# Two self-attention layers on one core: the softmax tiles of the first layer made in two halves of 512 queries

## The chip, the cores and the metric

The kernel runs on 1 core of a Trainium2 chip, in one launch. The metric is the device time of one execution in microseconds. TensorE multiplies matrices, ScalarE evaluates functions and copies, VectorE and GpSimd do elementwise work, and SyncE issues the DMAs. The engines run their own instruction streams and wait for each other only on semaphores.

## The reference

There are 8 images of 256 channels and 32 x 32 = 1024 positions, in fp32. Two layers follow each other, and each adds its result to its input:

```python
# layer 0 (q and k have 32 channels)
q = einsum('oc,bcn->bno', Wq, x) + bq
k = einsum('oc,bcn->bon', Wk, x) + bk
v = einsum('oc,bcn->bon', Wv, x) + bv
attn = softmax(einsum('bnc,bcm->bnm', q, k), axis=-1)
x = gamma * einsum('bcj,bij->bci', v, attn) + x
# layer 1 (256 channels), on the group norm h of x (32 groups)
attn = softmax(einsum('bct,bcs->bts', q(h), k(h)) / sqrt(256), axis=-1)
y = x + proj(einsum('bcs,bst->bct', v(h), attn))
```

## The kernel before

**Numbers.** Nearly every product is made of values split into a high part (`fp32r`) and a low part (the rest), as three matmuls that add into one bank: high x high, high x low, low x high (`three`, lines 597 to 599). The high part is written by ScalarE, the low part by VectorE, or by GpSimd for some operands.

**Layer 0.** An image has 8 tiles of 128 positions. In a first pass, `scores`, TensorE makes a 128 x 1024 tile of energies with queries on the partitions (line 607). VectorE takes each row's negated maximum (`row_max`, line 1067), and ScalarE the sum of the exponentials (`row_sums`, line 844), written back over the tile. From both comes one shift for each query (`log_sums`, `shifts`), which goes into two extra rows of the query matrix. In the second pass, `keys`, TensorE makes the tile again with keys on the partitions and the shift added (line 617), so that the exponential of it is already the transposed, normalised probability. This is a **keys tile**. ScalarE takes the exponential into `prob` (`exponent`, line 820) and copies it to `pt_hi` (`prob_hi`, line 834), and VectorE subtracts into `pt_lo` (`prob_lo`, line 1084), each over 1024 queries in one instruction. `prob` has 3 buffers, `pt_hi` and `pt_lo` have 4 each.

**Values.** `values` multiplies a tile's probabilities with 128 rows of v. It adds into four PSUM banks, numbered by `bank_of`: banks 0 and 1 are the two channel tiles for the first 512 queries, banks 2 and 3 those for the last 512. Each bank takes three matmuls.

**Layer 1.** Its tile, `logits`, is made once (12 matmuls). Its exponential has a row maximum as bias and gives the row sum. High and low part are scaled by the row's inverse.

**PSUM.** `ring` has four slots of 1024 columns. Slots 2 and 3 are the four banks of `values`. Slots 0 and 1 are handed round among everything else: keys, scores and logits tiles, and the projections `qk`, `value0`, `query` and `value1`. A table worked out at the start gives each entry its slot and the entry that had it before (`BEFORE`). Ahead of a fill, `wait_read` waits until that earlier entry has been read. For a keys tile this is the semaphore `keys_exp`, for scores `scores_exp`, for `query` `query_split`.

**Order.** `STEPS` is written by hand. A step has at most one tile, the `values` of a tile two steps back, and other entries. TensorE fills the step's tile, then its `early` entries, then makes the first `banks_first` banks of `values`, fills the `sides`, makes the remaining banks, and fills the `late` entries. Images 2 to 7 are made in one turn of 16 steps each, `turn(i)`: 8 keys tiles of image i, then 8 logits tiles of image i - 1. In steps 4 to 7 of a turn, where there is a next image, the order on TensorE is: keys tile, scores tile of image i + 1, banks 0 and 1, then one projection of image i - 1 (`query` 0 and 1, `value1` 0 and 1), then banks 2 and 3. The keys and scores tiles take the two slots, and the projection takes the slot of that step's keys tile. Step 3 makes `qk` of the next image right after its keys tile, in the slot of the keys tile of step 2. ScalarE's order in a step is: keys tile (exponential, copy), early entries (`row_sums`), sides, late entries. In step 1 it also makes the high part of layer 1's input (`hidden`, line 810).

The lines that decide when a slot is free, of `fill` and `reader`:

```python
if before and not (kind == before[0] == "weights"):
    wait_read(before)
...
"scores": ("scores_exp", image * TILES + m + 1),
"keys": ("keys_exp", image * TILES + m + 1),
"qk": ("qk_split", image * 2 + m + 1),
```

Of the kernel before, what the change touches and what calls it, by code (L numbers as in the profile page):

```python
# [6 lines left out]
F32 = mybir.dt.float32  # L7
F32R = mybir.dt.float32r
ACT = mybir.ActivationFunctionType
# [4 lines left out]
CT = C // P  # L14
TILES = N // P
# [6 lines left out]
PROBS = 3  # L22
PT = 4
# [194 lines left out]
RING_NO, SLOT, BEFORE, TILE_NO, PHASE_NO = {}, {}, {}, {}, {}  # L218
# [24 lines left out]
TILE_OF = list(TILE_NO)  # L243
# [23 lines left out]
def values_done(tile):  # L267

    kind, image, k = tile
    phase = PHASE_NO[int(kind == "logits"), image]  # L270
    if k == TILES - 1:
        return "pv_ready", phase * BANKS + BANKS
    return "tile_done", phase * (TILES - 1) + k + 1
# [1 line left out]

SEMAPHORES = (
    "ring_ready", "scores_max", "scores_exp", "log_ready", "shift_ready", "shift_read",
    "keys_exp", "logits_max", "logits_exp", "inv_ready", "p_hi", "p_split", "tile_done",
    "pv_ready", "pv_read", "query_half", "qk_hi", "qk_split", "value0_taken", "value0_kept", "value0_first", "value0_hi", "value0_split", "query_hi", "query_split",
    "v1_full", "v1_hi", "value1_split", "stats_ready", "norm_read", "coef_ready", "h_full", "h_hi", "h_split",  # L280
    "x_hi", "x_split", "res0_ready", "res1_ready", "weights_read", "weights_split", "rows_ready", "bias_read",
# [4 lines left out]
def build(nc, x, wqk_t, bqk, bk0, wv0_t, bv0, gamma, norm_w, norm_b, wq, bq, wk, bk, wv, bv, wp_t, bp,  # L286
          ident, group, y):
    with ExitStack() as ctx:
        def sb(name, shape, dt=F32):
            return ctx.enter_context(nc.sbuf_tensor(name, shape, dt))  # L290
# [16 lines left out]
        prob = sb("prob", [P, PROBS, N])  # L307
        pt_hi = [sb(f"pt_hi{j}", [P, N], F32R) for j in range(PT)]
        pt_lo = [sb(f"pt_lo{j}", [P, N], F32R) for j in range(PT)]
        neg_max = sb("neg_max", [P, 2])  # L310
        neg_raw = sb("neg_raw", [P, 2])
        row_sum = sb("row_sum", [P, 2])
        row_inv = sb("row_inv", [P, 2])
# [42 lines left out]
        ring = ctx.enter_context(nc.psum_tensor("ring", [P, 4, N], F32))  # L356
# [36 lines left out]
        def value1_split(i, k):  # L393

            if i == LAST:
                return [v[k // 4][:].rearrange("p (k c) -> p k c", c=C)[:, k % 4:] for v in (q4, k4)]
            return v1_hi[:, k:], v1_lo[:, k:]

        S = {name: ctx.enter_context(nc.semaphore(name)) for name in SEMAPHORES}
# [10 lines left out]
        half_cols = [slice(half * HALF, (half + 1) * HALF) for half in range(HALVES)]  # L410
# [167 lines left out]
        def _(pe):  # L578
            mm = nc.tensor.matmul

            def wait(name, n):
                pe.wait_ge(S[name], n)

            def wait_read(entry):

                for got in [entry] + GUESTS.get(entry, []):
                    wait(*reader(got))
                    if got[0] == "qk":
                        wait("key_hi", 2 * got[1] + got[2] + 1)
# [6 lines left out]
            def three(out, w_hi, w_lo, m_hi, m_lo, first, last):  # L596
                mm(out, w_hi, m_hi, start=first, stop=False)  # L597
                mm(out, w_hi, m_lo, start=False, stop=False)  # L598
                return mm(out, w_lo, m_hi, start=False, stop=last)  # L599
# [150 lines left out]
            def values(tile, banks):  # L750
                layer, i, k = tile
                p, phase = TILE_NO[("keys", "logits")[layer], i, k], PHASE_NO[layer, i]
                v_hi, v_lo = value1_split(i, k) if layer else (v0_hi[:, k:], v0_lo[:, k:])
                if k % 2 == 0 and 0 in banks:
                    if layer == 1:
                        wait("value1_split", 4 * i + k // 2 + 1)
                    elif i == 0:
                        wait("value0_first", k // 2 + 1)
                    else:
                        wait("value0_split", 4 * i + k // 2 - 3)  # L760
                if 0 in banks:
                    wait("p_split", p + 1)
                for b in banks:
                    half, ct = bank_of[b]
                    before = BEFORE[layer, i, 2 + b // 2] if k == 0 else None
                    if before and before[0] == "phase":
                        wait("pv_read", before[1] * BANKS + b + 1)
                    elif before and b % 2 == 0:
                        wait_read(before)
                    w, cols = slice(ct * P, (ct + 1) * P), half_cols[half]  # L770
                    last = three(pv_ps[:, b], v_hi[:, 0, w], v_lo[:, 0, w], pt_hi[p % PT][:, cols],
                                 pt_lo[p % PT][:, cols], k == 0, k == TILES - 1)
                    if k == TILES - 1:
                        last.then_inc(S["pv_ready"], 1)
                    elif b == BANKS - 1:
                        last.then_inc(S["tile_done"], 1)
# [17 lines left out]
        def _(act):  # L794
            copy, activation = nc.scalar.copy, nc.scalar.activation
# [17 lines left out]
            def exponent(tile):  # L813
                kind, i, k = tile
                p, slot = TILE_NO[tile], SLOT[tile]
                if p >= PROBS:
                    act.wait_ge(S["p_split"], p - PROBS + 1)
                if kind == "keys":
                    act.wait_ge(S["ring_ready"], RING_NO[tile] + 1)
                    activation(prob[:, p % PROBS], ring[:, slot], ACT.Exp).then_inc(S["keys_exp"], 1)  # L820
                else:
                    act.wait_ge(S["logits_max"], i * TILES + k + 1)
                    activation(prob[:, p % PROBS], ring[:, slot], ACT.Exp, bias=neg_max[:, k % 2:k % 2 + 1],  # L823
                               accum_out=row_sum[:, k % 2:k % 2 + 1]).then_inc(S["logits_exp"], 1)

            def prob_hi(tile):
                kind, i, k = tile
                p = TILE_NO[tile]
                if p >= PT:
                    name, n = values_done(TILE_OF[p - PT])  # L830
                    act.wait_ge(S[name], n)
                if kind == "keys":
                    act.wait_ge(S["keys_exp"], i * TILES + k + 1)
                    copy(pt_hi[p % PT][:], prob[:, p % PROBS]).then_inc(S["p_hi"], 1)  # L834
                else:
                    act.wait_ge(S["inv_ready"], i * TILES + k + 1)
                    activation(pt_hi[p % PT][:], prob[:, p % PROBS], ACT.Identity,  # L837
                               scale=row_inv[:, k % 2:k % 2 + 1]).then_inc(S["p_hi"], 1)

            def row_sums(entry):  # L840
                _, i, k = entry
                slot = SLOT[entry]
                act.wait_ge(S["scores_max"], i * TILES + k + 1)
                activation(ring[:, slot], ring[:, slot], ACT.Exp, bias=neg_max0[:, k:k + 1],  # L844
                           accum_out=row_sum0[:, k:k + 1]).then_inc(S["scores_exp"], 1)
# [5 lines left out]
            def shift_rows(entry):  # L851
                _, i, _ = entry
                act.wait_ge(S["ring_ready"], RING_NO[entry] + 1)
                copy(q4[i % 2][96:98], ring[0:2, SLOT[entry]]).then_inc(S["shift_read"], 1)
# [45 lines left out]

            def follow(entry):
                if entry[0] == "keys":
                    exponent(entry)
                    prob_hi(entry)
                elif entry[0] == "scores":
                    row_sums(entry)
                elif entry[0] == "shift":
                    shift_rows(entry)
                else:
                    project_hi(entry)  # L910
# [33 lines left out]
        def _(dve):  # L944
            V = nc.vector
# [11 lines left out]
            scale = C ** -0.5  # L957
# [120 lines left out]
            def prob_lo(tile):  # L1078
                kind, i, k = tile
                p = TILE_NO[tile]  # L1080
                hi, lo, src = pt_hi[p % PT], pt_lo[p % PT], prob[:, p % PROBS]
                dve.wait_ge(S["p_hi"], p + 1)
                if kind == "keys":
                    V.tensor_tensor(lo[:], src, hi[:].bitcast(F32), ALU.subtract).then_inc(S["p_split"], 1)  # L1084
                else:
                    dve.wait_ge(S["inv_ready"], i * TILES + k + 1)
                    V.scalar_tensor_tensor(lo[:], src, row_inv[:, k % 2:k % 2 + 1], hi[:].bitcast(F32), ALU.mult,  # L1087
                                           ALU.subtract).then_inc(S["p_split"], 1)
# [43 lines left out]
            def follow(entry):  # L1132
                if entry[0] == "keys":
                    prob_lo(entry)
                elif entry[0] == "scores":
                    row_max(entry)
                elif entry[0] == "norm":
                    norm(entry)
                else:
                    project_lo(entry)  # L1140
# [95 lines left out]
```

## Time and profile before

| | |
|---|---|
| time, median of 3 runs | 789.38 us (786.51 to 790.51) |
| time of the profiled execution | 785.61 us |
| its span | 783.8 us |
| TensorE busy | 774.1 us (99%), 3816 matmuls |
| VectorE busy | 554.7 us (71%), 806 instructions |
| ScalarE busy | 470.7 us (60%), 619 instructions |
| GpSimd busy | 163.8 us (21%) |
| mean granted clock of TensorE | 0.998 |

The span runs from the first instruction to the last; the time includes what lies around it. A matmul's row shows its time through the array, so rows overlap: the distance between two starts tells what one costs in the stream. An idle time in brackets is the engine's own, and the name behind the arrow is what ended it.

### The profile page before, as it was taken

Reading aid. Unit: us, or ns where it says so; the run is one execution under the profiler, and the core shown is the slowest. Engines: PE = TensorE matmul, PEld = TensorE weight load, DVE = VectorE, ACT = ScalarE, POOL = GpSimd, SP = SyncE. Lnnn points to the kernel's source line nnn. Section 1 sums busy time; section 2 is a strip of 40 time slices with the busy share of each in tenths; the row PEclk is TensorE's granted clock in tenths of the full one; section 3 lists DMA queues with packets and bytes.
Section 4 is the critical chain, followed back from the end, with each engine's and each line's share of the span. In section 5 each row is a group of like instructions: output and inputs, shape, how many; then the busy total and the mean of one; then the engine's idle time right before and its main releaser. Section 6 shows DMA issues by size and latency. Waiting matters only on the chain.

```text
span 783.8 us, 9844 instructions
## 1 busy us (share of the span) xinstructions
PE 774.1 (99%) x3816; PEld 647.4 (83%) x3816; DVE 554.7 (71%) x806; ACT 470.7 (60%) x619; POOL 163.8 (21%) x147
## 2 busy tenths in 40 slices
PE   9899999999999999999999999999999999999998
PEld 8678888888888888888888888888888888888886
DVE  5966778787578875788657796677856765476664
ACT  4876566567555775467745586456855566345343
POOL 5730052023100331005110240102310024111120
PEclk9999999999999999999999999999999999999999
DMA  6010010002000110001100011000100000000101
GB/s 189 0 55 1 1 54 1 1 23 86 1 1 1 55 54 1 1 1 54 55 1 1 0 56 54 1 1 0 54 1 2 0 33 22 1 0 1 54 1 54
DMA packets 10365, 18.98 MB, mean 24 GB/s; under 512 B 2128, under 2 KB 3920, under 8 KB 10320
## 3 DMA queue, kind: packets, MB, share of 16 engines
q1 hardware_dynamic: 10320, 18.36, 6.8%
q8 instruction: 30, 0.49, 0.3%
q14 instruction: 15, 0.12, 0.1%
HBM read 9.97 MB, written 8.39 MB: 23 GB/s over the span
## 4 chain that ended last, share of the span: by engine, by line
PE 95%; ACT 2%; DVE 2%; issue 0%; POOL 0%; ACTq 0%; DVEq 0%; POOLq 0%
PE ring L597 29%; PE ring L599 28%; PE ring L598 28%; PE ring L617 4%; PE ring L607 3%; PE ring L594 1%; ACT ring L844 1%; ACT pt_hi L834 1%; ACT prob L820 1%; PE ring L636 1%; DVE neg_max L1067 0%; DVE res L1120 0%; DVE pt_lo L1084 0%; PE ring L691 0%; PE ring L716 0%
## 5 line engine op out<-in xcount | busy, mean ns | idle before, releaser
L597 PE MATMUL ring<-pt_hi,v_hi 128*128 128x512 f32 x480 | 189.4, 395 | 0.0
L599 PE MATMUL ring<-pt_hi,v_lo 128*128 128x512 f32 x480 | 188.5, 393 | 0.0
L598 PE MATMUL ring<-pt_lo,v_hi 128*128 128x512 f32 x480 | 188.3, 392 | 0.0
L823 ACT ACTIVATE prob<-ring,neg_max 128x1024 f32<-128x1024 f32 x64 | 71.5, 1118 | 155.1 <-DVE neg_max L1070 155.1
L1069 DVE TENSOR_REDUCE neg_raw<-ring 128x1 f32<-128x1024 f32 x64 | 78.2, 1222 | 58.0 <-PE ring L599 57.9
L504 POOL TENSOR_TENSOR v_lo<-v_f,v_hi 128x512 fp32r<-128x512 f32 x28 | 37.7, 1347 | 385.1 <-ACT v_hi L861 385.1
L1084 DVE TENSOR_TENSOR pt_lo<-prob,pt_hi 128x1024 fp32r<-128x1024 f32 x64 | 81.8, 1278 | 37.5 <-ACT pt_hi L834 37.3
L599 PEld LDWEIGHTS ring<-pt_hi,v_lo 128*128 128x128 f32 x480 | 90.3, 188 | 19.9
L597 PEld LDWEIGHTS ring<-pt_hi,v_hi 128*128 128x128 f32 x480 | 90.5, 188 | 18.4 <-issue 0.4
L598 PEld LDWEIGHTS ring<-pt_lo,v_hi 128*128 128x128 f32 x480 | 90.6, 189 | 18.2
L1067 DVE TENSOR_REDUCE neg_max<-ring 128x1 f32<-128x1024 f32 x64 | 77.7, 1223 | 35.4 <-PE ring L607 35.3
L844 ACT ACTIVATE ring<-ring,neg_max 128x1024 f32<-128x1024 f32 x64 | 69.4, 1084 | 39.9 <-DVE neg_max L1067 39.8
L1087 DVE SCALAR_TENSOR_TENSOR pt_lo<-prob,row_inv,pt_hi 128x1024 fp32r<-128x1024 f32 x64 | 83.1, 1298 | 8.6 <-ACT pt_hi L837 8.4
L597 PE MATMUL ring<-h_hi,query_hi 128*128 128x512 f32 x224 | 88.0, 393 | 0.0
L598 PE MATMUL ring<-h_lo,query_hi 128*128 128x512 f32 x224 | 87.5, 391 | 0.0
L599 PE MATMUL ring<-h_hi,query_lo 128*128 128x512 f32 x224 | 87.5, 391 | 0.0
L820 ACT ACTIVATE prob<-ring 128x1024 f32<-128x1024 f32 x64 | 65.5, 1024 | 36.4 <-PE ring L617 36.2
L837 ACT ACTIVATE pt_hi<-prob,row_inv 128x1024 fp32r<-128x1024 f32 x64 | 73.7, 1152 | 9.6 <-DVE row_inv L1076 9.3
L834 ACT CAST pt_hi<-prob 128x1024 fp32r<-128x1024 f32 x64 | 67.3, 1051 | 5.3
L599 PEld LDWEIGHTS ring<-h_hi,query_lo 128*128 128x128 f32 x224 | 42.0, 188 | 8.9
L597 PEld LDWEIGHTS ring<-h_hi,query_hi 128*128 128x128 f32 x224 | 42.1, 188 | 8.8 <-ACT prob L823 0.2
L598 PEld LDWEIGHTS ring<-h_lo,query_hi 128*128 128x128 f32 x224 | 42.1, 188 | 8.6
(167 smaller groups left out, 1346.8 us busy)
## 6 DMA issues: line engine op xcount, KB each, us to landing
out_y<-res SPq DMA_DIRECT2D x32, 256.0 KB, 2.2
x_in<-in_x SPq DMA_DIRECT2D x7, 1024.0 KB, 4.9
x_in<-in_x SPq DMA_DIRECT2D x2, 512.0 KB, 5.2
h_f<-in_wv_t SPq DMA_DIRECT2D x1, 256.0 KB, 4.4
res<-in_wq SPq DMA_DIRECT2D x1, 256.0 KB, 6.8
res<-in_wk SPq DMA_DIRECT2D x1, 256.0 KB, 7.1
res<-in_wv SPq DMA_DIRECT2D x1, 256.0 KB, 7.6
res<-in_wp_t SPq DMA_DIRECT2D x1, 256.0 KB, 7.1
```

The source lines that it names most:

```text
L597: mm(out, w_hi, m_hi, start=first, stop=False)
L598: mm(out, w_hi, m_lo, start=False, stop=False)
L599: return mm(out, w_lo, m_hi, start=False, stop=last)
L820: activation(prob[:, p % PROBS], ring[:, slot], ACT.Exp).then_inc(S["keys_exp"], 1)
L823: activation(prob[:, p % PROBS], ring[:, slot], ACT.Exp, bias=neg_max[:, k % 2:k % 2 + 1], accum_out=row_sum[:, k % 2:k % 2 + 1]).then_inc ...
L834: copy(pt_hi[p % PT][:], prob[:, p % PROBS]).then_inc(S["p_hi"], 1)
L837: activation(pt_hi[p % PT][:], prob[:, p % PROBS], ACT.Identity, scale=row_inv[:, k % 2:k % 2 + 1]).then_inc(S["p_hi"], 1)
L844: activation(ring[:, slot], ring[:, slot], ACT.Exp, bias=neg_max0[:, k:k + 1], accum_out=row_sum0[:, k:k + 1]).then_inc(S["scores_exp"], 1)
L1067: V.tensor_reduce(neg_max0[:, k:k + 1], src, AX_X, ALU.max, negate=True).then_inc(S["scores_max"], 1)
L1069: link(V.tensor_reduce(neg_raw[:, k % 2:k % 2 + 1], src, AX_X, ALU.max, negate=True))
L1084: V.tensor_tensor(lo[:], src, hi[:].bitcast(F32), ALU.subtract).then_inc(S["p_split"], 1)
L1087: V.scalar_tensor_tensor(lo[:], src, row_inv[:, k % 2:k % 2 + 1], hi[:].bitcast(F32), ALU.mult, ALU.subtract).then_inc(S["p_split"], 1)
```

## The change

A keys tile is no longer made in three instructions of 1024 queries, but in six of 512. ScalarE takes the exponential of the first half (signal `keys_half`), waits for it, copies the first half (`half_hi`), takes the exponential of the second half (`keys_exp`), waits for it, and copies the second half (`p_hi`). VectorE subtracts the first half after `half_hi` (`half_split`) and the second after `p_hi` (`p_split`). TensorE waits for `half_split` ahead of bank 0 and for `p_split` ahead of bank 2. The slot is still given back by `keys_exp`, which is now the second half's exponential. Layer 1's tiles are made as before.

```diff
@@ TensorE, values
-                if 0 in banks:
-                    wait("p_split", p + 1)
                 for b in banks:
                     half, ct = bank_of[b]
+                    if layer == 0 and b == 0:
+                        wait("half_split", i * TILES + k + 1)
+                    elif b == (0 if layer else CT):
+                        wait("p_split", p + 1)
@@ ScalarE, in place of exponent and prob_hi for keys tiles
+            def keys_probs(tile):
+
+                _, i, k = tile
+                p, slot = TILE_NO[tile], SLOT[tile]
+                if p >= PROBS:
+                    act.wait_ge(S["p_split"], p - PROBS + 1)
+                act.wait_ge(S["ring_ready"], RING_NO[tile] + 1)
+                for half, cols in enumerate(half_cols):
+                    part = prob[:, p % PROBS][:, cols]
+                    done = ("keys_half", "keys_exp")[half]
+                    activation(part, ring[:, slot][:, cols], ACT.Exp).then_inc(S[done], 1)
+                    if half == 0 and p >= PT:
+                        name, n = values_done(TILE_OF[p - PT])
+                        act.wait_ge(S[name], n)
+                    act.wait_ge(S[done], i * TILES + k + 1)
+                    copy(pt_hi[p % PT][:, cols], part).then_inc(S[("half_hi", "p_hi")[half]], 1)
@@ ScalarE, follow
                 if entry[0] == "keys":
-                    exponent(entry)
-                    prob_hi(entry)
+                    keys_probs(entry)
@@ VectorE, prob_lo
-                dve.wait_ge(S["p_hi"], p + 1)
                 if kind == "keys":
-                    V.tensor_tensor(lo[:], src, hi[:].bitcast(F32), ALU.subtract).then_inc(S["p_split"], 1)
+                    for half, cols in enumerate(half_cols):
+                        if half == 0:
+                            dve.wait_ge(S["half_hi"], i * TILES + k + 1)
+                        else:
+                            dve.wait_ge(S["p_hi"], p + 1)
+                        V.tensor_tensor(lo[:, cols], src[:, cols], hi[:, cols].bitcast(F32),
+                                        ALU.subtract).then_inc(S[("half_split", "p_split")[half]], 1)
                 else:
+                    dve.wait_ge(S["p_hi"], p + 1)
```

## Rows read from the trace of the kernel before

**Rows 1.** The page's head, engine sums and granted clock over 40 slices.

```profile
span 783.8 us, 9844 instructions
...
PE 774.1 (99%) x3816; PEld 647.4 (83%) x3816; DVE 554.7 (71%) x806; ACT 470.7 (60%) x619; POOL 163.8 (21%) x147
...
PEclk9999999999999999999999999999999999999999
```

**Rows 2.** Waits of TensorE: waiter, releaser, total us, times, longest; eight lines.

```profile
PE ring L607 <- ACT ring L844: 2.7, 5, 1.5
...
PE ring L607 <- ACT prob L820: 0.4, 1, 0.4
...
PE ring L617 <- DVE v_lo L1019: 0.3, 1, 0.3
```

**Rows 3.** ScalarE by line and form: busy us, mean ns, idle before.

```profile
L834 ACT CAST pt_hi<-prob 128x1024 fp32r<-128x1024 f32 x64 | 67.3, 1051 | 5.3
L820 ACT ACTIVATE prob<-ring 128x1024 f32<-128x1024 f32 x64 | 65.5, 1024 | 36.4 <-PE ring L617 36.2
...
L861 ACT CAST v_hi<-v_f 128x512 fp32r<-128x512 f32 x28 | 17.3, 619 | 25.7 <-DVE v_f L997 25.7
...
L876 ACT CAST v_hi<-ring 128x512 fp32r<-128x512 f32 x28 | 16.4, 587 | 3.2 <-PE ring L599 3.2
```

**Rows 4.** VectorE by line and form, same columns.

```profile
L1084 DVE TENSOR_TENSOR pt_lo<-prob,pt_hi 128x1024 fp32r<-128x1024 f32 x64 | 81.8, 1278 | 37.5 <-ACT pt_hi L834 37.3
...
L1019 DVE TENSOR_TENSOR v_lo<-ring,v_hi 128x512 fp32r<-128x512 f32 x28 | 19.3, 689 | 8.3 <-ACT v_hi L876 8.3
```

**Rows 5.** Timeline of TensorE, step 4 of turn 3: start, duration, instruction.

```profile
277.28 0.63 PE L617 MATMUL ring<-q,k 98*128 98x512 f32 x2
277.74 0.63 PE L607 MATMUL ring<-k,q 96*128 96x512 f32 x2
278.21 0.40 PE L597 MATMUL ring<-pt_hi,v_hi 128*128 128x512 f32 x1
...
279.59 0.40 PE L597 MATMUL ring<-h_hi,wqq_hi 128*128 128x512 f32 x1
```

**Rows 6.** Timeline of ScalarE, the same step.

```profile
278.00 1.03 ACT L820 ACTIVATE prob<-ring 128x1024 f32<-128x1024 f32 x1 [1.17 <-PE ring L617]
279.12 1.05 ACT L834 CAST pt_hi<-prob 128x1024 fp32r<-128x1024 f32 x1
280.08 1.07 ACT L844 ACTIVATE ring<-ring,neg_max 128x1024 f32<-128x1024 f32 x1
```

**Rows 7.** Timeline of TensorE, the same step of turn 6.

```profile
559.98 0.63 PE L617 MATMUL ring<-q,k 98*128 98x512 f32 x2
...
562.29 0.40 PE L597 MATMUL ring<-h_hi,wqq_hi 128*128 128x512 f32 x1
```

**Rows 8.** Timeline of turn 3, steps 1 to 3: ScalarE, then TensorE's fill of qk.

```profile
266.91 1.03 ACT L820 ACTIVATE prob<-ring 128x1024 f32<-128x1024 f32 x1 [0.39 <-PE ring L617]
...
268.98 2.37 ACT L810 ACTIVATE h_hi<-x,norm_c,norm_a 128x1024 fp32r<-128x1024 f32 x2
271.26 1.00 ACT L820 ACTIVATE prob<-ring 128x1024 f32<-128x1024 f32 x1
...
273.12 0.40 PE L597 MATMUL ring<-x_hi,wqk_hi 128*128 128x512 f32 x1
```

**Rows 9.** Timeline of TensorE in image 0, fills that wait.

```profile
40.38 0.73 PE L607 MATMUL ring<-k,q 96*128 96x512 f32 x2 [1.46 <-ACT ring L844]
...
48.98 0.73 PE L617 MATMUL ring<-q,k 98*128 98x512 f32 x2
...
58.30 0.73 PE L617 MATMUL ring<-q,k 98*128 98x512 f32 x2 [0.26 <-DVE v_lo L1019]
...
62.45 1.20 PE L607 MATMUL ring<-k,q 96*128 96x512 f32 x4 [0.21 <-ACT ring L844]
```

More of the change, by code:

```diff
@@ L277 @@
     "ring_ready", "scores_max", "scores_exp", "log_ready", "shift_ready", "shift_read",
-    "keys_exp", "logits_max", "logits_exp", "inv_ready", "p_hi", "p_split", "tile_done",
+    "keys_half", "keys_exp", "half_hi", "half_split", "logits_max", "logits_exp", "inv_ready", "p_hi", "p_split", "tile_done",
     "pv_ready", "pv_read", "query_half", "qk_hi", "qk_split", "value0_taken", "value0_kept", "value0_first", "value0_hi", "value0_split", "query_hi", "query_split",
@@ L817, in exponent @@
                     act.wait_ge(S["p_split"], p - PROBS + 1)
[L818 to L824, printed above, removed]
+                act.wait_ge(S["logits_max"], i * TILES + k + 1)
+                activation(prob[:, p % PROBS], ring[:, slot], ACT.Exp, bias=neg_max[:, k % 2:k % 2 + 1],
+                           accum_out=row_sum[:, k % 2:k % 2 + 1]).then_inc(S["logits_exp"], 1)
             def prob_hi(tile):
@@ L831, in prob_hi @@
                     act.wait_ge(S[name], n)
[L832 to L838, printed above, removed]
+                act.wait_ge(S["inv_ready"], i * TILES + k + 1)
+                activation(pt_hi[p % PT][:], prob[:, p % PROBS], ACT.Identity,
+                           scale=row_inv[:, k % 2:k % 2 + 1]).then_inc(S["p_hi"], 1)
+            def keys_probs(tile):
[13 more added lines that the diff above has]
+                    copy(pt_hi[p % PT][:, cols], part).then_inc(S[("half_hi", "p_hi")[half]], 1)
             def row_sums(entry):
```

## Prediction

> **What bounds the kernel now.** I read the page's head first, then the waits of TensorE, then the timeline of one step, and last the groups by form. TensorE is busy for 774.1 of 783.8 us, and its clock is at the top in every slice [rows 1]. The waits view gives it 6.5 us of idle time in all (the sum of its eight lines), the largest item 2.7 us, nearly all of it before 63 us and behind ScalarE's `row_sums` [rows 2]. From then on TensorE issues one 512-column matmul every 0.23 us (start to start, though each row shows 0.39 us, since they overlap) with hardly a hole [rows 5]. So nothing can be gained but those few microseconds, and any new hole in TensorE's stream is paid in full at the end: the stream has no idle time later in which it could be caught up. ScalarE (60% busy) and VectorE (71%) [rows 1] are not bounds by their sums. What matters is *when* they give something back to TensorE. The question is therefore which of TensorE's waits are met only just in time, and how far the change moves them.
>
> **What the values gain.** `values` runs two steps behind its tile. In the step at 277.28 it multiplies with tile 2 of the image, whose exponential began at 271.26 [rows 5, 8]; with 1.00 + 0.09 + 1.05 us on ScalarE and 1.2 us on VectorE its low part was there by about 275, 3 us before use. No row of the waits has TensorE wait at L597 to L599 for a low part [rows 2]. So the early half signal releases something nobody waits for: gain 0. The second wait, in front of bank 2, has the two later banks and all that follows queued behind it, but the last low half comes at about the same time as the whole one did (below): cost 0, cover 3 us.
>
> **What one tile costs on ScalarE.** A 1024-column copy from SBUF takes 1.051 us, a 512-column one 0.619; a 512-column copy out of PSUM takes 0.587, the 1024-column exponential 1.024 [rows 3]. The first two give 0.43 us for 512 columns and 0.19 us fixed. So a half exponential takes 0.60 (1.024 - 0.43) and a half copy 0.62. Between an exponential and the copy that waits for it lie 0.09 us (279.12 - 279.03), and an instruction that waits for nothing of ScalarE begins 0.09 us before the end of the one ahead (280.08 against 280.17) [rows 6]. Before, from the start of the exponential to the next instruction: 2.08 us [rows 6]. After: 0.60 + 0.09 + 0.62 - 0.09 + 0.60 + 0.09 + 0.62 - 0.09 = 2.44, which I take as **+0.35 us** per tile.
>
> **When the ring slot comes free.** This is the term that decides. The tile's slot is given back by `keys_exp`, and that now comes with the *second* half exponential, which stands behind the *first* half copy. Before: 1.03 us after the start of the exponential. After: 0.60 + 0.09 + 0.62 - 0.09 + 0.60 = 1.82. The release comes **0.79 us later**, 0.62 of it the copy put in between and the rest the second fixed cost. Bounds: 0.70 (no gap before the copy) and 0.96 (no overlap at either joint: 1.99 less 1.03).
>
> **VectorE.** A 1024-column subtraction takes 1.278 us, a 512-column one 0.689 [rows 4]: two make 1.38, +0.1 us where VectorE is behind. Where it waits for ScalarE it does the first half early; the last half then ends 2.5 (last copy) + 0.03 + 0.69 = 3.2 us after the start, against 1.03 + 0.09 + 1.05 + 0.03 + 1.22 = 3.4 before. So `p_split` comes 0.2 us earlier there: gain 0, by the 3 us of cover. Queued behind it are `row_max` and the low parts of the projections, which gain or lose 0.1 us, and ScalarE's `row_sums` follows later than that anyway.
>
> **Steps 4 to 7 of each turn** (`turn(i)`, images 2 to 6, which have scores and a next image). TensorE fills tile k at 277.28, fills scores, runs two banks, and at 279.59 fills the query projection, into *the slot of tile k* [rows 5]. That is 2.31 us after the fill began. The exponential begins at 278.00 and ended at 279.03 [rows 6]: slack 0.56, of which 0.04 passes between release and use (TensorE began that soon after a release where it had waited). After: 278.00 + 1.82 + 0.04 = 279.86, a **stall of 0.27 us**. All four steps are alike (query 0 and 1, value1 0 and 1 take the slot of keys 4, 5, 6, 7), and the last turn has the same times (559.98 to 562.29) [rows 7]. One stall doesn't soften the next, since the next exponential waits for a fill that comes as much later: ScalarE waited 1.17 us for it [rows 6], more than the 0.35 that it loses. 5 turns x 4 x 0.27 = **5.4 us**; by the bounds of the release (0.18 and 0.44 each) 3.6 to 8.8.
>
> **Step 3 of these turns.** `qk` of the next image takes the slot of tile 2 at 273.12; that exponential ran from 271.26 to 272.26, slack 0.86. It is itself late by ScalarE's queue: keys 0's lengthening goes into the 0.39 us of idle time before keys 1, but keys 1's doesn't, since `hidden` (L810) and keys 2 follow without a gap [rows 8]. So the exponential begins 0.35 later and gives back 0.79 later: 0.35 + 0.79 - 0.86 + 0.04 (+ 0.02, it was a 1.00 us one) = **0.34 us**, five times, **1.7 us** (bounds 0.2 and 0.55: 1.0 to 2.8). ScalarE is then 1 us behind and its parts of `qk` come so much later; scores at 277.74 need them and VectorE's part behind them, which I make out at 0.1 us ahead of TensorE. Nothing added.
>
> **Image 0.** Here ScalarE sets the pace. The fills at 48.98, 58.30 and 62.45 wait, at the end of a chain, for what ScalarE did behind the tile's copy (a projection's copy and its low part, `row_sums`) [rows 9]. The lengthening passes through at each: 3 x 0.35 = **1.0 us**. Ahead of them scores 1 comes up to 1.1 us later (its slot is that of tile 1), but that goes into the 1.46 us for which TensorE idles at 40.38, whose end hangs on VectorE's maximum. Bounds 0.5 (half of it hidden) to 2.1 (the 1.1 not hidden). **Image 1** has one tight place, the fill of its first query behind VectorE's low part of the values; I take 0.1. In the last turn no scores stand between tile and projection, so the projection takes the slot of the tile before, a whole step older (3 us or more against 0.79): 0.
>
> **Sum:** 5.4 + 1.7 + 1.0 + 0.1 = **8.2 us**, bounds 5.2 and 13.8. The profiled execution took 785.6 us (span 783.8 and 1.8 around it), so 793.8, +1.04%. The three timed runs have their median at 789.4, 3.8 above it; on that footing 797.6, which I give, with a range of the likeliest case of 794.6 to 803.2.
>
> **A rule weighed.** The rows put the fixed cost of one ScalarE instruction at 0.19 us [rows 3]. The Trainium skill, "ScalarE: Activation LUTs", section "What ACT_TABLE_LOAD costs", gives 186 ns plus 0.833 ns a column, and 93 ns of overlap back to back: it speaks against cutting such instructions, and the rows agree. It has no term for the wait of a copy on the exponential ahead of it; by it alone the release would move by 3 x 0.613 - 0.093 - 1.039 = 0.71 us, an estimate from that page, and the sum would be about 6 us.
>
> **The rivals.**
> *A, not slower: the slack swallows it.* The slot's release moves by less than 0.52 us, so that steps 4 to 7 and step 3 stay whole. It decides at 0.52. For it: the slack is there, the clean places keep 0.56. Against: 0.62 us of copy lie in between, whatever the halves cost. Only if the half copy took under 0.35 us would it hold. Then image 0 alone is left: 789.4 + 0.8 = 790.2. Chance 0.09.
> *B, the early half pays.* VectorE, done 0.2 us earlier, shortens the stalls before 63 us. All of TensorE's waits are 6.5 us, those in reach (40.38, 58.30, 62.45) 1.9 [rows 9]; with the stalls of steps 4 to 7 absent as in A: 789.4 - 1.5 = 787.9. Against: ScalarE, not VectorE, ends those chains. Chance 0.04.
> *C, larger: the joints cost more.* Each self-wait of ScalarE costs 0.2 us instead of 0.09, and step 3's lateness reaches the scores behind it: release +1.0, 20 x 0.48 + 5 x 0.9 + 2 = 16 us, 805. Nothing in the rows shows such a gap. Chance 0.05.
> The likeliest has 0.82.
>
> **How the numbers follow.** Predicted 797.6. The range, 792 to 803.5, holds nearly all of the likeliest case with a microsecond or two for the base, and leaves A, B and the far end of C out. 0.5% is 3.9 us, about what this measurement can tell from no change. Slower by more: the likeliest nearly whole (its lower bound is 5.2 us) and C, 0.85. Within: A, most of B and a rest, 0.13. Faster: 0.02.
>
> **What would show it.** L820 and L834 with 128 rows each, near 0.60 and 0.62 us; ScalarE's busy time up by some 22 us, VectorE's by 6. In steps 4 to 7 the first matmul of query and value1 0.49 us after the one ahead instead of 0.23, in step 3 0.57; the waits view shows less (0.1 and 0.2 each, as the row of the matmul ahead covers 0.16), now with TensorE waiting for `prob` in 25 places. Turns of images 2 to 6 longer by 1.4 us each, the last turn and the end unchanged. It is wrong if those intervals stay at 0.23 us, if the waits move to scores, or if the clock falls because of the holes: then every matmul costs more and the sum is too small.

## The result and the profile after

The changed kernel takes 799.69 us (median of 4 runs, 796.9 to 800.24) against 788.64 for the kernel before (median of 4, 786.51 to 790.51). The ratio is 1.0134, 95% interval 1.0098 to 1.017: slower by about 11 us, or 1.3%. Forecast were 797.6 us, and 8.2 us more than before. The profiled execution took 800.24 us. Later executions of the kernel before, timed with the experiments, have medians of 786.8 to 787.1 us, so the 11 us may be one or two too little; the interval reaches 13.4. Two executions, one of 1559 us in experiment 1 and one of 1983 us in experiment 8, were disturbed and are left out of the ratios below.

The page's head, engine sums and chain of the changed kernel, which answer to [rows 1]:

```profile
span 798.4 us, 10044 instructions
...
PE 783.2 (98%) x3816; PEld 647.2 (81%) x3816; DVE 567.7 (71%) x870; ACT 487.7 (61%) x747; POOL 161.2 (20%) x147
...
PE 82%; ACT 11%; DVE 4%; issue 1%; ACTq 0%; POOL 0%; DVEq 0%; POOLq 0%
```

ScalarE has 128 instructions and 17 us more, VectorE 64 and 13 us more. TensorE does the same 3816 matmuls and is "busy" for 9.1 us longer. That is no work: a matmul's row covers 0.39 us and the next one normally starts 0.23 us after it, so up to 0.16 us of every hole in the stream counts as busy. (A second stretch at the lower clock, below, adds to it.) The chain is the honest view here. ScalarE has 11% of it, 2% before.

The half instructions by line and form, of ScalarE and VectorE:

```profile
L849 ACT CAST pt_hi<-prob 128x512 fp32r<-128x512 f32 x128 | 79.5, 621 | 7.4
L844 ACT ACTIVATE prob<-ring 128x512 f32<-128x512 f32 x128 | 75.9, 593 | 30.5 <-PE ring L617 29.0 <-DVE pt_lo L1098 0.7
...
L1098 DVE TENSOR_TENSOR pt_lo<-prob,pt_hi 128x512 fp32r<-128x512 f32 x128 | 94.7, 758 | 21.8 <-ACT pt_hi L849 21.3
```

0.593 and 0.621 us on ScalarE are the 0.60 and 0.62 that were worked out from [rows 3]. VectorE's 0.758 is more than the 0.689 of [rows 4].

TensorE's waits in the changed kernel, against [rows 2]:

```profile
PE ring L607 <- ACT ring L855: 2.8, 5, 1.3
PE ring L607 <- ACT prob L844: 1.4, 1, 1.4
PE ring L636 <- DVE shift_pair L1110: 1.4, 1, 1.4
PE ring L597 <- DVE v_lo L1029: 1.3, 1, 1.3
```

The holes of steps 3 to 7 are not in this view at all: what is left of each after the 0.39 us row is 0.1 us of idle time. They have to be read off the timeline. Step 4 of turn 3 on TensorE, against [rows 5]:

```profile
284.99 0.63 PE L617 MATMUL ring<-q,k 98*128 98x512 f32 x2
285.46 0.62 PE L607 MATMUL ring<-k,q 96*128 96x512 f32 x2
...
287.08 0.39 PE L599 MATMUL ring<-pt_hi,v_lo 128*128 128x512 f32 x1
287.58 0.50 PE L597 MATMUL ring<-h_hi,wqq_hi 128*128 128x512 f32 x1
287.91 0.39 PE L598 MATMUL ring<-h_lo,wqq_hi 128*128 128x512 f32 x1
```

and the same stretch on ScalarE, against [rows 6]:

```profile
285.72 0.60 ACT L844 ACTIVATE prob<-ring 128x512 f32<-128x512 f32 x1 [0.72 <-PE ring L617]
286.40 0.62 ACT L849 CAST pt_hi<-prob 128x512 fp32r<-128x512 f32 x1
286.93 0.59 ACT L844 ACTIVATE prob<-ring 128x512 f32<-128x512 f32 x1
287.55 0.63 ACT L849 CAST pt_hi<-prob 128x512 fp32r<-128x512 f32 x1
```

The second exponential ends at 287.52, 1.80 us after the first began, and the query projection's first matmul starts at 287.58, 0.50 us after the one ahead of it instead of 0.23: a hole of 0.27. The next matmul follows after 0.33 us instead of 0.23, since the first one behind a hole takes 0.50 instead of 0.40. So a hole costs **0.37 us**, not 0.27. From keys fill to projection it is 2.59 us (2.31 before), and at all twenty places of steps 4 to 7 the two starts lie 0.49 to 0.52 us apart. Value1's shorter matmuls pay the 0.10 behind the hole as well.

Where the profiled execution's 14.6 us more lie, by the starts of keys fills (L617), in us:

| stretch | before | after | more |
|---|---|---|---|
| start to first keys fill | 30.35 | 32.30 | 1.95 |
| images 0 and 1, to keys tile 0 of image 2 | 138.36 | 141.96 | 3.60 |
| turns 2 to 6, to keys tile 0 of image 7 | 469.75 | 478.79 | 9.04 |
| from there to the end | 145.37 | 145.38 | 0.01 |
| one turn (step 4 of turn 3 to turn 6, by 3) | 94.23 | 96.04 | 1.81 |

The first line is code that the change doesn't touch. In the 13 profiles that are read here, in all of which that stretch is the same code, the first keys fill starts between 30.35 and 32.62 us, so the medians' 11 us is the better figure for the change.

Much of that spread goes with TensorE's granted clock. The views by window of the kernel before and then of the changed kernel (busy us of PE, PEld, DVE, ACT and POOL with their instructions, then the granted clock as a share of 2.4 GHz):

```profile
21.90:25.30 3.40, 3.09 (x20) 2.45 (x19) 2.85 (x4) 2.77 (x7) 2.39 (x3) 1.00 0.00 0
75.70:79.10 3.40, 3.40 (x9) 2.63 (x9) 3.30 (x10) 2.23 (x3) 0.00 (x0) 0.50 0.00 0
```

```profile
21.90:25.30 3.40, 3.40 (x15) 3.21 (x15) 1.98 (x2) 3.23 (x6) 1.58 (x2) 0.51 0.00 0
80.00:83.40 3.40, 3.40 (x12) 2.92 (x11) 3.37 (x7) 2.37 (x5) 0.00 (x0) 0.50 0.00 0
```

The kernel before ran for 3.4 us at 1.2 GHz, with 512-column matmuls 0.43 us apart instead of 0.23. The changed kernel did so twice. Ahead of them TensorE had been busy without a break (from 70.0 to 75.7 us before and from 74.0 to 80.0 us in the changed kernel), and for 5.14 of the 6.90 us from 15.0 to 21.9 us in the changed kernel. The later stretches of the two kernels cancel. In the one at 21.9 the changed kernel falls from 0.5 to 2.0 us behind. Five of the 13 profiles have a stretch near 22 us, among them those of experiments 3 and 5, and in them the first keys fill starts at 32.30 to 32.62; in the eight others it starts at 30.35 to 31.75. The turns, where the loss of the change lies, ran at the upper level in both kernels.

### The profile page after: what moved, and what is told of

Same layout as the page of the kernel before. It is cut to its first block, busy times and chain, and to the rows that moved or that the text cites. A ratio compares the mean times of both kernels' runs of the same rounds, so it can differ in the third digit from the quotient of the medians.

```text
span 798.4 us, 10044 instructions
## 1 busy us (share of the span) xinstructions
PE 783.2 (98%) x3816; PEld 647.2 (81%) x3816; DVE 567.7 (71%) x870; ACT 487.7 (61%) x747; POOL 161.2 (20%) x147
## 4 chain that ended last, share of the span: by engine, by line
PE 82%; ACT 11%; DVE 4%; issue 1%; ACTq 0%; POOL 0%; DVEq 0%; POOLq 0%
PE ring L597 26%; PE ring L599 25%; PE ring L598 25%; ACT prob L844 5%; ACT pt_hi L849 3%; PE ring L617 3%; PE ring L607 2%; ACT h_hi L812 1%; PE ring L594 1%; ACT ring L855 1%; DVE pt_lo L1098 1%; DVE neg_max L1077 1%; DVE h_lo L980 0%; DVE k L1041 0%; DVE k L1042 0%
## 5 line engine op out<-in xcount | busy, mean ns | idle before, releaser
L1098 DVE TENSOR_TENSOR pt_lo<-prob,pt_hi 128x512 fp32r<-128x512 f32 x128 | 94.7, 758 | 21.8 <-ACT pt_hi L849 21.3
L844 ACT ACTIVATE prob<-ring 128x512 f32<-128x512 f32 x128 | 75.9, 593 | 30.5 <-PE ring L617 29.0
L849 ACT CAST pt_hi<-prob 128x512 fp32r<-128x512 f32 x128 | 79.5, 621 | 7.4
```

The lines of the kernel that those rows point to most:

```text
L844: activation(part, ring[:, slot][:, cols], ACT.Exp).then_inc(S[done], 1)
L849: copy(pt_hi[p % PT][:, cols], part).then_inc(S[("half_hi", "p_hi")[half]], 1)
L1098: V.tensor_tensor(lo[:, cols], src[:, cols], hi[:, cols].bitcast(F32), ALU.subtract).then_inc(S[("half_split", "p_split")[half]], 1)
```

## The experiments

Twelve kernels ran, each timed against the kernel before on the same chip. "Turn" is the length of one turn, read as in the table above: it is free of the start's spread. 94.23 is before, 96.04 the changed kernel.

Where a difference in us stands beside a ratio, it is that ratio less 1, times the median of the kernel before; the medians themselves lie up to 2 us further apart (18.4 instead of 16.7 us in experiment 2, 7.9 instead of 5.8 in experiment 4).

**1. Exponentials first.** The same six instructions on the same halves, in another order on ScalarE:

```diff
                 for half, cols in enumerate(half_cols):
+                    activation(prob[:, p % PROBS][:, cols], ring[:, slot][:, cols],
+                               ACT.Exp).then_inc(S[("keys_half", "keys_exp")[half]], 1)
...
+                for half, cols in enumerate(half_cols):
+                    act.wait_ge(S[("keys_half", "keys_exp")[half]], i * TILES + k + 1)
+                    copy(pt_hi[p % PT][:, cols],
+                         prob[:, p % PROBS][:, cols]).then_inc(S[("half_hi", "p_hi")[half]], 1)
```

> Halves as in the changed kernel, but ScalarE takes both half exponentials first and then makes both half copies. Release theory (the loss comes from the slot that is given back 0.79 us later): the release comes 0.60 - 0.09 + 0.60 = 1.11 us after the start instead of 1.82, within the slack of 0.52, so the holes of steps 3 to 7 vanish: within 1.5 us of the kernel before. ScalarE theory (the loss comes from six instructions where there were three, 17 us more of busy time on ScalarE): busy time is the same as in the changed kernel, so +11 us as there.

Measured: ratio 1.0014 (0.9994 to 1.0034), turn 94.25 us. The same instructions cost nothing that shows once the slot is given back ahead of the copies. Its step 4 on ScalarE and then TensorE:

```profile
280.72 1.09 ACT L842 ACTIVATE prob<-ring 128x512 f32<-128x512 f32 x2 [1.23 <-PE ring L617]
281.83 1.15 ACT L849 CAST pt_hi<-prob 128x512 fp32r<-128x512 f32 x2
282.88 1.08 ACT L856 ACTIVATE ring<-ring,neg_max 128x1024 f32<-128x1024 f32 x1
```

```profile
279.99 0.63 PE L617 MATMUL ring<-q,k 98*128 98x512 f32 x2
...
282.07 0.39 PE L599 MATMUL ring<-pt_hi,v_lo 128*128 128x512 f32 x1
282.30 0.40 PE L597 MATMUL ring<-h_hi,wqq_hi 128*128 128x512 f32 x1
```

Both exponentials take 1.09 us together, and from their start to the next instruction it is 2.16 us (2.08 before, 2.44 by the forecast for the changed kernel and 2.36 as measured there): where nothing waits for the instruction just ahead, the joints cost hardly anything. The projection follows 0.23 us behind the values, without a hole. So this run takes away the late release and most of ScalarE's lengthening at once: ScalarE is busy for 474.9 us in it, against 487.7 in the changed kernel and 470.7 before, and not for the same time, as I had expected. It clears the number of instructions alone; the next four runs tell release and length apart.

**2. The release alone.** The kernel before, whole instructions, with the slot given back by the copy:

```diff
-        "keys": ("keys_exp", image * TILES + m + 1),
+        "keys": ("p_hi", TILE_NO.get(entry, 0) + 1),
```

> The kernel before, whole instructions, but a keys tile's slot is given back only by the copy to pt_hi, 1.14 us later. Release theory: steps 4 to 7 stall by 1.14 - 0.52 = 0.62 and 0.10 for the first matmul behind a hole, 20 x 0.72 = 14.4; step 3 by 0.32 + 0.10, five times, 2.1; image 0 about 1.7: +18 us against before. ScalarE theory: its work is that of the kernel before, so +0 to 2.

Measured: ratio 1.0212 (1.0172 to 1.0252), +16.7 us; turn 97.56, +3.33 against 3.30 forecast (4 x 0.72 + 0.42). Not one instruction that computes differs from before. Here a hole is long enough to show:

```profile
283.59 0.63 PE L617 MATMUL ring<-q,k 98*128 98x512 f32 x2
...
285.68 0.39 PE L599 MATMUL ring<-pt_hi,v_lo 128*128 128x512 f32 x1
286.53 0.50 PE L597 MATMUL ring<-h_hi,wqq_hi 128*128 128x512 f32 x1 [0.46 <-ACT pt_hi L834]
```

0.85 us between the starts, 0.62 more than 0.23; the idle column shows 0.46 of it.

**3. Whole exponential, halves behind it**, and **4. the same with the slot given back by the first half copy** (a smaller dose):

```diff
-                    activation(part, ring[:, slot][:, cols], ACT.Exp).then_inc(S[done], 1)
+                activation(prob[:, p % PROBS], ring[:, slot], ACT.Exp).then_inc(S["keys_exp"], 1)
...
-        "keys": ("keys_exp", image * TILES + m + 1),
+        "keys": ("half_hi", image * TILES + m + 1),
```

(The first two lines are in both, the last two in the fourth alone.)

> One exponential of 1024 queries, then the copy and the subtraction in two halves. Release theory: the slot comes free as before, ScalarE's work for a tile is 0.1 us longer: +0 to 1 against before. Rival, that instruction counts cost something in themselves (64 more on ScalarE, 64 more on VectorE): +4 or more.

> As the run with the whole exponential, but the slot is given back by the first half copy, 0.71 us later than before instead of 0.79. Release theory: steps 4 to 7 stall by 0.71 - 0.52 = 0.19 and 0.10 behind it, 20 x 0.29 = 5.8, step 3 about 0, image 0 0.7: +6.5 against before. ScalarE theory: as the run with the whole exponential, +0 to 1.

Measured: the third 1.001 (0.9991 to 1.0028), turn 94.23; the fourth 1.0074 (1.0049 to 1.0098), +5.8 us, turn 95.53, +1.30 (forecast were 4 x 0.29 = 1.16; its timeline has 4 x 0.30, and in step 3 no hole but the 0.10 behind one). Between these two kernels only one semaphore's name differs. A release later by 0, 0.71, 0.79 (the changed kernel) and 1.14 us, as worked out ahead of the runs, gives turns longer by 0, 1.30, 1.81 and 3.33 us.

**5. ScalarE longer, release as before.** Two copies of 96 columns into a spare buffer behind each keys tile's copy:

```diff
...
                     copy(pt_hi[p % PT][:], prob[:, p % PROBS]).then_inc(S["p_hi"], 1)
+                    for j in range(2):
+                        copy(spare[:, j], ones[:, 0:96])
...
```

> The kernel before, and behind each keys tile's copy ScalarE makes two more copies of 96 columns into a spare buffer that nobody reads, together about 0.36 us, the lengthening of the changed kernel, with the release left as it was. Release theory: only image 0 (1.0) and at most 0.5 elsewhere: +1 to 1.5 against before. ScalarE theory: +8 to 11.

Measured: 1.0053 (1.0036 to 1.007), +4.2 us, turn 94.92. A miss for my theory as I put it, which allowed 1.5, and for its rival, which wanted 8. The turns of images 2 to 6 hold 3.4 us more than before. The timeline has the holes in step 4, ahead of scores:

```profile
280.54 0.68 ACT L889 ACTIVATE q<-ring,bqk_s 64x512 fp32r<-64x512 f32 x1
```

```profile
281.26 0.74 DVE L1043 SCALAR_TENSOR_TENSOR q<-ring,bqk_s,q 32x512 fp32r<-32x512 f32 x1 [0.55 <-ACT q L889]
```

```profile
281.42 0.63 PE L618 MATMUL ring<-q,k 98*128 98x512 f32 x2
...
282.25 0.70 PE L608 MATMUL ring<-k,q 96*128 96x512 f32 x2 [0.20 <-DVE q L1043]
```

ScalarE's lateness of step 3 goes through `qk` to VectorE and to the scores, which start 0.25 us after VectorE's part has ended (281.26 + 0.74). In the changed kernel the same lateness is there, but TensorE itself is held by 0.37 at `qk`, so that the scores come just late enough: 0.40 us after that part. That was the "nothing added, 0.1 us ahead" of the forecast: right, but by that little. So ScalarE's length is not free, and with the release as before it would cost 0.4 to 0.8 us a turn at another place.

**6. TensorE waits for the whole tile** in the changed kernel:

```diff
-                    if layer == 0 and b == 0:
-                        wait("half_split", i * TILES + k + 1)
-                    elif b == (0 if layer else CT):
+                    if b == 0:
                         wait("p_split", p + 1)
```

> The changed kernel, but TensorE waits for the whole tile (p_split) ahead of bank 0 again, as before; the half signal is unused. My step (nobody waits for the half): same as the changed kernel within 1 us, +11 against before. Rival, that the early half wins something which the loss covers: slower than the changed kernel by 2 us or more.

Measured: 1.0155 (1.0124 to 1.0185), 800.85 us, turn 96.10 against 96.04. The intervals of the two ratios overlap. The two profiles, which have the same two stretches at the lower clock, settle it better: spans of 798.7 and 798.4 us. The half signal is worth nothing that shows.

**7, 8 and 9. By image:** halves in images 2 to 7, in images 0 and 1, and in image 0. The other tiles are made whole, with the code of the kernel before. The condition is the one below, or `< 2`, or `== 0`:

```diff
+HALVED = [tile for tile in TILE_OF if tile[0] == "keys" and tile[1] >= 2]
```

> Halves as in the changed kernel, but only for the tiles of images 2 to 7; images 0 and 1 have whole tiles. Release theory: 25 holes of 0.27 + 0.10 us: +9.2 against before, and images 0 and 1 hold the rest of the 11. Rival, that image 0, where ScalarE sets the pace, holds most of the loss: +3 or less.

> Halves only for the tiles of images 0 and 1. Release theory: +1 to 2.5 against before (1.0 of image 0, and the hole at the first query of image 1, 1.5 us in the profile after, if it is not chance). Rival, that image 0 holds most of the loss: +8 or more. A gain here, -0.5 or lower, would say that the early half pays where TensorE idles.

> Halves only for the tiles of image 0. My step for image 0: ScalarE's lengthening passes three times, and the holes behind keys_exp bring a first matmul that costs 0.10 more: +1.0 to 1.5 against before. Rival, that the 1.1 us by which scores 0 of image 1 comes later is not taken up by the hole behind it: +2 or more.

Measured: 1.0109 (1.0063 to 1.0155), turns 2 to 6 together 478.98, +9.2; 1.003 (1.001 to 1.0049), +2.4 us; 1.0033 (1.0022 to 1.0045), +2.6 us. By time the first two make 8.6 and 2.4, together the changed kernel's 11. Of the eighth only the times are used.

The ninth is a miss: I had expected 1.0 to 1.5, and the rival 2 or more. Its profile has 1.7 us more in image 0, 1.0 of them ahead of scores 0 of image 1, where the idle time behind did not take them up, as the rival said. It also has a hole of 1.06 us (and 0.10 behind it) ahead of the first query of image 1, though the tiles of that image are whole. That hole is what the next run is about; in the changed kernel it is 1.51 us.

**10. Two tiles.** Halves only for tiles 6 and 7 of image 1 (`HALVED` with those two).

> Halves only for the last two tiles of image 1, all others whole. It asks for the hole of 1.5 us at the first query of image 1, which the profiles of the changed kernel, of the whole wait and of the longer ScalarE have, and four others with whole or late-released tiles have not. If ScalarE's 0.35 us a tile there pushes VectorE's low parts and h_lo under GpSimd's residuals (they run at twice the time there), the hole is in this profile: query 0 late by 1.5, +1.5 us against before. If it is chance of one execution or comes from further ahead: no hole, +0.

Measured: 1.0025 (1.0012 to 1.0038), about 2 us, and the hole (1.53 us) is in its profile. Two half-split tiles are enough for it. (The profile also has a stretch at the lower clock, 6.8 us long instead of 3.4, that ends at 82.5 us; the ten timed executions don't hang on it.) The same stretch of the kernel before and then of the changed kernel, on VectorE:

```profile
102.96 1.23 DVE L1084 TENSOR_TENSOR pt_lo<-prob,pt_hi 128x1024 fp32r<-128x1024 f32 x1 [1.17 <-ACT pt_hi L834]
104.11 1.22 DVE L1067 TENSOR_REDUCE neg_max<-ring 128x1 f32<-128x1024 f32 x1
105.24 2.35 DVE L970 TENSOR_TENSOR h_lo<-h_f,h_hi 128x1024 fp32r<-128x1024 f32 x2
```

```profile
105.98 2.64 DVE L1098 TENSOR_TENSOR pt_lo<-prob,pt_hi 128x512 fp32r<-128x512 f32 x2 [1.60 <-ACT pt_hi L849]
108.55 1.21 DVE L1077 TENSOR_REDUCE neg_max<-ring 128x1 f32<-128x1024 f32 x1
109.68 3.19 DVE L980 TENSOR_TENSOR h_lo<-h_f,h_hi 128x1024 fp32r<-128x1024 f32 x2
```

and on GpSimd in the changed kernel:

```profile
105.27 2.81 POOL L489 TENSOR_SCALAR res<-x,unit,bp_s 128x1024 f32<-128x1024 f32 x2
109.55 4.38 POOL L497 TENSOR_SCALAR x<-x_in,unit,gbv 128x1024 f32<-128x1024 f32 x2 [1.47 <-ACT h_hi L812]
```

and on GpSimd in the kernel before:

```profile
105.38 4.39 POOL L497 TENSOR_SCALAR x<-x_in,unit,gbv 128x1024 f32<-128x1024 f32 x2 [0.28 <-ACT h_hi L810]
```

`h_lo` and GpSimd's residual (L497) both wait for ScalarE's `h_hi` and lie over each other in either kernel. Before, VectorE was 0.14 us ahead and took 2.35 us for its two; after, GpSimd was 0.13 ahead and VectorE took 3.19. The line's own view, before and after, shows that it is one of the two instructions that grows (shortest, median and longest in ns):

```profile
L970 DVE TENSOR_TENSOR h_lo<-h_f,h_hi x2: 1216/1218/1219, 105.2 to 106.4; 128x1024 fp32r<-128x1024 f32 x2
```

```profile
L980 DVE TENSOR_TENSOR h_lo<-h_f,h_hi x2: 1208/1631/2054, 109.7 to 110.8; 128x1024 fp32r<-128x1024 f32 x2
```

All 13 profiles fit this. In six VectorE began first, by 0.09 to 0.48 us (the kernel before and experiments 1, 2, 3, 4 and 7), and the query has no hole. In seven GpSimd did, by 0.13 to 0.18 us and in experiment 9 by 0.8, and the query has one of 1.1 to 1.7 us. The halves of `pt_lo` ahead of it, also over GpSimd, take 1.3 us each on average and delay VectorE. The values' low part and the first query wait behind all this, and the query is 1.5 us late. So a race between two engines is lost by ScalarE's lengthening, or, as experiment 9 shows with whole tiles, by other small shifts ahead of it. That the order of the two starts decides it is read from the traces, not forced by an experiment.

**11 and 12. More work ahead of the slot's next use.** The changed kernel with three banks instead of two ahead of the projection, in steps 6 and 7 (value1), or, with `s in (4, 5)`, in steps 4 and 5 (query):

```diff
-            step.banks_first = 2 if s >= 4 else 1
+            step.banks_first = 3 if s >= 6 and has(i + 1) else 2 if s >= 4 else 1
```

> The changed kernel, but in steps 6 and 7 of the turns of images 2 to 6 TensorE makes three banks instead of two ahead of the value projection, 0.69 us more work between the keys fill and the next use of its slot. Release theory: the ten holes of 0.27 + 0.10 go, and at most 0.05 each comes back at v1_full (slack 0.65 before): 3 to 3.7 us faster than the changed kernel, about +7.7 against before. Rival, that the holes have another cause (ScalarE's load, the order of the banks): no change, +11.

> The same move in steps 4 and 5, where the projection is the query, whose split the next scores fill waits for with 0.17 us of slack. Release theory: the holes at keys_exp go, but the query comes 0.43 us later than in the changed kernel and the scores behind it wait 0.56 + 0.10, so that each step is 0.66 longer than before instead of 0.37: ten steps, 2.9 us slower than the changed kernel, about +14 against before. Rival (the extra bank simply hides the hole): 3.7 us faster than the changed kernel.

Measured: 1.0125 (1.0108 to 1.0142), 796.67 us, turn 95.41, 0.63 less than the changed kernel's; and 1.018 (1.0162 to 1.0199), 801.16 us, turn 96.29, 0.25 more. In the second the waits view has a new first line:

```profile
PE ring L607 <- DVE query_lo L1023: 4.0, 10, 0.4
```

Ten waits, as many as steps were changed. The holes at `keys_exp` went and came back, larger, at the scores. I had expected 0.58 a turn; it is 0.25, because the late scores of step 6 push that step's projection back, so that one of the holes behind it closes.

## Why the prediction was right, step by step

- **TensorE's stream is what counts, and a hole is paid in full:** right in the turns. 25 holes of 0.37 make 9.2, the turns are 9.04 longer, and from image 7 to the end nothing is caught up (0.01).
- **The values gain 0:** shown (experiment 6).
- **One tile on ScalarE, +0.35:** the halves came out at 0.593 and 0.621 us, but the tile at 0.29 more: where nothing is waited for it takes 2.36 us (274.27 to 276.63 in turn 3) against 2.07. The second copy starts 0.03 us behind its exponential and not 0.09 (287.52 to 287.55).
- **The slot 0.79 us later:** right to 0.02 in the profile (1.80 - 1.03), and shown to be the cause in the turns: moved alone it costs about what was forecast (3.33 a turn for 3.30 in experiment 2, 1.30 for 1.16 in 4 against 3), put back it is gone with all six instructions kept (1). The upper bound of 0.96 was added up wrongly: with a gap of 0.09 and no overlap the sum is 1.91, and the bound 0.88.
- **Steps 4 to 7, a stall of 0.27:** measured 0.27 to 0.29, twenty times. **The mis-sized term is what a hole costs:** I counted the waiting alone, and the first matmul behind it took another 0.10, which 25 times makes 2.5 us. The rows of before had it: fills that waited show 0.73 for a pair [rows 9], those that did not 0.63 [rows 5].
- **Step 3, 0.34:** measured 0.26 to 0.28 (0.50 us between the starts against 0.24), and 0.10 behind it. The stall was reckoned with ScalarE 0.35 us late; it was 0.29.
- **Image 0, 1.0, and image 1, 0.1:** too small; both together 3.6 in the profile, 2.4 by experiment 8. Image 0 has 1.7 of the 3.6, the first query of image 1 has 1.6, and a fill at 146.5 us has 0.3. In image 0 the three places named are not where it comes through: of them only 62.45 shows it (0.30), 48.98 shows nothing and 58.30 is 0.25 shorter; a value projection (46.00 before) and the scores at 53.23 have 0.38 and 0.30. The 1.1 us ahead of scores 0 of image 1 (1.0 measured) was to vanish in the idle time at 40.38, and did not: that idle time was still 1.3 us long afterwards (the waits above), because VectorE's first low parts, in halves, took 2.61 and 2.22 us a pair beside GpSimd, and the maximum behind them came later. In image 1 it was the same contention. That 1.0 lay within the bounds of 0.5 to 2.1 is in part luck.
- **VectorE +6 us:** it was 13, for this reason (0.758 a half, 0.689 forecast).
- **The waits view would show 25 places:** wrong, it showed none of them.
- **The clock at the top in every slice:** misread. The digit 9 of [rows 1] stands for 90% or more of a slice of 19.6 us, and 3.4 us at half clock hide in it. The sum doesn't hang on this.
- **Rivals.** A (slack swallows it): excluded, the release passed 0.52 us. B (the early half pays): no gain in experiments 6 and 8. C: the joints cost 0.09 and 0.03, not 0.2.
- **The number:** the difference is the fair measure, 8.2 forecast and 11 measured. By the times of experiments 7 and 8 the turns lack 1.5 (7.1 against 8.6) and images 0 and 1 lack 1.3 (1.1 against 2.4).

No version beat the kernel before: exponentials first and the whole exponential are even with it. Not tried: an order of GpSimd's residuals that keeps clear of image 1's low parts.

## What to carry to other kernels

When an instruction is cut in two so that its *output* is ready earlier, look at who waits for its *input buffer*: put the last reader of the buffer first and whatever else is to be done behind it. On a saturated engine, list for each buffer it refills the time between release and refill; here 0.56 us, repeated twenty times, decided 7.4 of the 11 us, and no view of busy time shows it. Count with each hole the 0.10 us by which the first matmul behind it came out longer here.

## What the runs showed of the hardware that was not expected

A 512-column matmul behind a hole of 0.27 us or of 0.62 us alike took 0.50 us instead of 0.40, and its successor started 0.10 us later than in the running stream. Behind the holes of 0.20 us of experiment 4 the successor was 0.10 us later too.

VectorE's subtraction of two SBUF operands can be held up for as long as an instruction of GpSimd runs. In the changed kernel the halves of `pt_lo` are spread widely (ns, shortest, median, longest):

```profile
L1098 DVE TENSOR_TENSOR pt_lo<-prob,pt_hi x128: 672/685/1766, 34.9 to 685.9; 128x512 fp32r<-128x512 f32 x128
```

Of these 128, 91 overlap no instruction of GpSimd and take 0.67 to 0.69 us. Of the 37 others 22 take 0.68 to 0.70 and 15 take 0.92 to 1.77. Each of those 15 ended 0.53 to 0.55 us after the GpSimd instruction that was running when it began had ended, whatever it had waited; the stretched subtractions of 1024 columns, in all profiles, ended 1.06 to 1.08 us after it. The other side pays likewise: a GpSimd instruction of 1.2 us (L497) took 3.21 in the kernel before, over the two `h_lo`. The Trainium skill, "Trainium Architecture — The Big Picture" section "What this means for kernel authors", says that within the engines' side of SBUF only the shared port pair of VectorE and GpSimd contends, as an exclusive lock. The traces agree, and show one side held until the other's instruction has ended.
